# Where a transformer kernel writes its rows of ones, who casts its first two weight slots, and its last four input loads

## What is computed

```
x = x + attn_a(layernorm(x));  x = x + ffn(layernorm(x))
x = x + attn_b(layernorm(x));  x = x + ffn(layernorm(x))
# attn: softmax(causal(q k^T / sqrt(32))) v, 16 heads of 32, then a 512 x 512 projection
# ffn:  (silu(x w_gate^T) * (x w_up^T)) w_down^T, hidden 2048
```

## Time and profile before

| | us |
|---|---|
| median of 3 runs | 2128.01 |
| lowest, highest | 2127.96, 2130.42 |
| the profiled execution | 2130.63 |
| its span, first to last instruction | 2128.9 |
| PE busy | 2062.0 (97%) |
| DVE busy | 1210.9 (57%) |
| POOL busy | 999.1 (47%) |
| ACT busy | 698.6 (33%) |
| store of a tile, issue to landing, median | 2.1 |

### The profile page before, as it was taken

The page is one execution under the profiler, slowest core; times in us unless marked ns, Lnnn a source line. Parts: engine busy times, 40 slices in busy tenths (PEclk is TensorE's granted clock), DMA queues, the critical chain, the costliest instruction groups (busy, mean ns, idle before and its releaser), DMA issues.

```text
span 2128.9 us, 35275 instructions
## 1 busy us (share of the span) xinstructions
PE 2062.0 (97%) x10816; PEld 1443.1 (68%) x10816; DVE 1210.9 (57%) x2452; ACT 698.6 (33%) x1348; POOL 999.1 (47%) x776
## 2 busy tenths in 40 slices
PE   6999999999999999999999999999999999999997
PEld 5555478888755547888875554888877554588886
DVE  6766554454676645544557664555456666454554
ACT  1344432231144443222214444222221444422321
POOL 3323249863312425975331242697533223379752
PEclk9999999999999999999999999999999999999999
DMA  4433101111323210211242321111113232111112
GB/s 129 101 78 83 32 30 50 60 60 40 81 71 81 71 31 30 64 51 55 70 131 71 81 71 31 40 60 50 50 41 85 66 81 71 41 39 62 50 57 92
DMA packets 59756, 135.18 MB, mean 63 GB/s; under 512 B 10784, under 2 KB 11808, under 8 KB 59552
## 3 DMA queue, kind: packets, MB, share of 16 engines
q1 hardware_dynamic: 59552, 132.71, 22.1%
HBM read 77.62 MB, written 4.19 MB: 38 GB/s over the span
## 4 chain that ended last, share of the span: by engine, by line
PE 86%; issue 4%; DVE 3%; POOL 3%; ACT 2%; DMA 1%; SPq 0%; DVEq 0%; POOLq 0%; ACTq 0%
PE bank L1279 13%; PE bank L1166 10%; PE bank L1168 10%; PE bank L1167 10%; PE ring L1166 9%; PE ring L1167 9%; PE ring L1168 9%; PE ring L1233 8%; PE bank L1257 7%; PE ring L1157 1%; POOL area L671 1%; ACT prob L713 1%; DMA area<-nm_lo 1%; POOL area L530 1%; DVE xn L908 1%
## 5 line engine op out<-in xcount | busy, mean ns | idle before, releaser
L713 ACT ACTIVATE prob<-bank 128x512 f32<-128x512 f32 (+3 forms) x768 | 335.0, 489 | 343.6 <-PE bank L1257 342.8
L908 DVE CUSTOM_DVE_ANT_0 xn<-ring,mask_row 128x128 bf16<-128x128 f32 (+7 forms) x512 | 374.8, 749 | 106.4 <-PE ring L1233 99.5
L605 POOL TENSOR_SCALAR_AFFINE_SELECT prob<-prob 128x512 f32<-128x512 f32 x128 | 84.1, 657 | 568.7 <-ACT prob L713 568.7
L528 POOL TENSOR_SCALAR area<-w_stage 128x1024 fp32r<-128x1024 f32 x131 | 149.9, 1144 | 369.3 <-PE bank L1168 194.7
L530 POOL TENSOR_TENSOR area<-w_stage,area 128x1024 fp32r<-128x1024 f32 x131 | 313.9, 2396 | 10.9
L967 DVE TENSOR_TENSOR x<-x,bank 128x512 f32<-128x512 f32 x256 | 170.8, 684 | 233.1 <-PE bank L1168 233.1
L1166 PE MATMUL ring<-xt_hi,area 128*128 128x512 f32 x688 | 273.7, 398 | 4.3 <-DVE xt_lo L880 2.8
L1167 PE MATMUL ring<-xt_lo,area 128*128 128x512 f32 x688 | 269.3, 391 | 0.0
L1168 PE MATMUL ring<-xt_hi,area 128*128 128x512 f32 x688 | 268.9, 391 | 0.0
L1233 PE MATMUL ring<-area 96*128 96x512 f32 (+3 forms) x768 | 239.1, 372 | 9.4 <-DVE row_max L908 8.4
L1233 PEld LDWEIGHTS ring<-area 96*128 96x128 f32 x768 | 131.1, 188 | 151.1 <-DVE row_max L908 94.5
(11 more groups left out here) (144 smaller groups left out, 3233.6 us busy)
## 6 DMA issues: line engine op xcount, KB each, us to landing
w_stage<-ffn_w SPq DMA_DIRECT2D x96, 512.0 KB, 3.3
area<-kq_parts SPq DMA_DIRECT2D x336, 128.0 KB, 2.4
w_stage<-attn_w SPq DMA_DIRECT2D x35, 512.0 KB, 3.2
x<-x_in SPq DMA_DIRECT2D x24, 256.0 KB, 3.9
area<-attn SPq DMA_DIRECT2D x48, 128.0 KB, 2.3
out<-x SPq DMA_DIRECT2D x16, 256.0 KB, 2.1
bias_rows<-row_bias SPq DMA_DIRECT2D x10, 256.0 KB, 4.2
area<-nm_hi SPq DMA_DIRECT2D x32, 8.0 KB, 1.8
```

Of the source, the lines that this page charges most:

```text
L528: pool.tensor_scalar(hi, src, 1.0, 0.0, ALU.mult, ALU.add).then_inc(w_hi_done, 1)
L713: act.activation(prob[:, step % 2, h, off:], bank[n % 2][:, off:], ACT.Exp, scale=SCALE).then_inc(prob_ready, 1)
L908: dve.tensor_tensor_reduce(out=sum_out[:, RING[name] % 2, 0:keys], in0=src[:, 0:keys], in1=mask_row[:, TOKENS - keys:], scale=1.0, scalar= ...
```

## The change

Three edits. **Ones:** VectorE's memset at the start and both memsets of GpSimd are gone; instead GpSimd writes all four buffers with one memset at the head of each iteration, right behind the `rstd` of tiles 4 to 7, for which it waits, and ahead of the split of slot 3. **First two slots:** ScalarE casts their high parts before the loop; GpSimd subtracts the low parts, and only once `xn_ready` says that tiles 0 to 3 are normalised; TensorE waits for slot 0 and slot 1 apart, each where it first uses it. **Input:** the four loads of chunk 1 behind the last batch are gone, SP's outer loop is written out, and SP waits for the stores at its end.

```
-            with sp.Fori(0, BATCH) as b:
+            for b in range(BATCH):
...
-                        if n >= AFTER_STORE:
+                        if n >= AFTER_STORE and not (b == BATCH - 1 and c):
...
-            for s in x_loaded:
-                sp.wait_ge(s, 16 * CT * (BATCH + 1))
+            for c, s in enumerate(x_loaded):
+                sp.wait_ge(s, 16 * CT * (BATCH + 1 - c))
+            for s in x_stored:
+                sp.wait_ge(s, 16 * BATCH)
...
-            split_weights(0, 0)
             inverse_deviation(0, 0, 0)
-            for i in range(1, AHEAD):
+            wait_alone(pool, xn_ready, CT)
+            for i in V_SLOTS:
+                hi, lo = w_part(i, slice(0, SLOT))
+                wait_alone(pool, w_hi_done, i + 1)
+                pool.tensor_tensor(lo, w_stage[:, i, :], hi.bitcast(F32), ALU.subtract).then_inc(w_split, 1)
+            for i in range(len(V_SLOTS), AHEAD):
                 split_weights(0, i)
             with pool.Fori(0, BATCH * LAYERS) as it:
                 inverse_deviation(it, 0, 1)
+                wait_alone(pool, rstd_ready, it * 2 * CHUNKS + CHUNKS)
+                pool.memset(k_stack[3 * HEAD:3 * HEAD + 2, :, :, :].bitcast(F32), 1.0).then_inc(ones_ready, 1)
+                pool.wait_ge(ones_ready, it + 1)
                 split_weights(it, AHEAD)
...
-                pool.memset(k_stack[3 * HEAD:3 * HEAD + 2, 0, :, :].bitcast(F32), 1.0).then_inc(ones_ready, 1)
-                pool.wait_ge(ones_ready, 2 * it + 2)
...
-                wait_alone(pool, product_full, products(it, QUAD_LAST, "m3", 1))
-                wait_alone(pool, w_split, it * SLOTS + SLOTS + 2)
-                pool.memset(k_stack[3 * HEAD:3 * HEAD + 2, 1:, :, :].bitcast(F32), 1.0).then_inc(ones_ready, 1)
-                wait_alone(pool, ones_ready, 2 * it + 3)
...
+            for i in V_SLOTS:
+                act.wait_ge(w_loaded[i], 16)
+                act.activation(w_part(i, slice(0, SLOT))[0], w_stage[:, i, :], ACT.Copy).then_inc(w_hi_done, 1)
...
-            dve.memset(k_stack[3 * HEAD:3 * HEAD + 2, 1:, :, :].bitcast(F32), 1.0).then_inc(ones_ready, 1)
...
-                        pe.wait_ge(w_split, it * SLOTS + V_SLOTS[1] + 1)
+                    if k % 2 == 0:
+                        pe.wait_ge(w_split, it * SLOTS + V_SLOTS[k // 2] + 1)
...
-                        if u in (0, 2):
-                            pe.wait_ge(ones_ready, 2 * it + 1 + u // 2)
+                        if u == 0:
+                            pe.wait_ge(ones_ready, it + 1)
```

## The result

The changed kernel takes 2139.34 us (2138.56 to 2140.64, 6 runs) against 2129.22 us of the kernel before (2127.96 to 2131.87, 6 runs): ratio 1.0045, 95% interval 1.0034 to 1.0056, so some 10 us slower. Its profiled execution has a span of 2137.2 us, 8.3 more than that of before.

A forecast was written before the change was run, and what follows sets the result against it. TensorE's matmuls bound the kernel (86% of the chain), so only its waits count. Heads +27.6, start -5.7 and end -5.0 us make +16.9 on a median of 2128.0: 2145 us, range 2116 to 2150.

The forecast's parts named there:

- The hold: Iteration heads: VectorE's normalisation waits for GpSimd's whole memset, key projection 10.0 us behind the start of `xn`; chance 0.72.
- The clock: Iteration heads: TensorE's clock falls behind the waits, +2.1 us each in iterations 1 and 3, 1.0 in iteration 0.
- The start: Before the first product: normalisation without GpSimd beside it lets that product start at 16.35 instead of 22.04, -5.7 us.
- The end: End of the program: the last store follows at once instead of behind a load, -5.0 us.
- The sum: Whole kernel: 27.6 - 5.7 - 5.0 = +16.9 us, so 2145 us.
- Rival (1): Iteration heads: the memset does not hold VectorE up, as it reads nothing; only the gains stand, 2117.3 us; chance 0.20.
- Rival (2): Heads: held, but one tile passes first and the clock stays up in iterations 0, 1, 3; 2138 us; no separate chance.
- Rival (3): Heads: TensorE gets only the transposes late and something else loses its wait, loss of 6 to 15 us; chance 0.05.
- rival (4): Start: the gain fails, slot 1's low part or ScalarE's cast being late; at most 5.7 us back, 2151; chance 0.03.

The follow-up runs named there:

- e1: The changed kernel, but GpSimd's memset of ones waits until tiles 4 to 7 are normalised; 2115.73 us, ratio 0.9936 to the kernel before.
- e3: The changed kernel, but VectorE normalises tiles 4 to 7 with a two-tensor scalar_tensor_tensor, memset still behind rstd; 2120.71 us, ratio 0.9951 to the kernel before.
- e10: The changed kernel with half of the memset behind rstd and the other half behind the normalisation; 2127.31 us, ratio 0.9989 to the kernel before.
- e4: The kernel before with the edit on the ones alone; 2151.45 us, ratio 1.0095 to the kernel before.

## Why the prediction was right, and where it was off

**The hold.** Right, and shown by e1, e3 and e10: the first `tensor_scalar` waits for the whole memset and 0.28 us more. The 10.0 us from the start of `xn` to the key projection is 9.98 in iterations 0, 1 and 3 and 9.96 in iteration 2 (562.11 - 552.13 in iteration 1). The losses of time alone were forecast as 3.4, 6.1, 6.8 and 6.1; by the distances they are 3.4, 6.1, 6.7 and 5.6. The last is smaller because iteration 3 of before does not repeat iteration 1: its key projection starts 4.4 us behind `xn`, not 3.9.

**The clock.** The term that was mis-sized, with iteration 2. For iterations 1 and 3 I took 2.1 us each from iteration 2 of before; they took 1.5. For iteration 0 I took 1.0: there was none, although TensorE waited 1.85 and 1.07 us there; behind the same waits in e4 it was 1.5, so the half that I took is not refuted. In iteration 2 the twelve matmuls took 4.08 us instead of 4.94, so the clock came back sooner than before, behind a longer wait. I had 5.2 us for the clock, and the traces give 0 + 1.5 - 0.9 + 1.6 = 2.2. I had also held fixed what VectorE waits for ahead of `xn`: in iteration 2 it waited 2.91 us for its input instead of 3.83, and in iteration 1 `xn` came 0.4 us earlier against TensorE than before. The heads cost 22.7 us by the traces, 23.6 by the medians against e1, and I had 27.6.

**The start.** -6.8 instead of -5.7. The first product came 5.0 us earlier and not 5.7; 0.4 of that is the input, which landed at 7.0 and not 6.6. Another 1.8 us came from the full clock of the first nine matmuls, which I had left out. That part is luck: e3 has the same start, its first matmuls ran at the lower clock, and it is 5.05 us ahead in the second value tile, where e1 is 7.0. That ScalarE's casts and the later subtractions are hidden was right (1.06 us each).

**The end.** -5.2 for -5.0.

**The sum.** +16.9 was forecast, +9.6 measured by the ratio; the terms by the traces, 22.7 - 6.8 - 5.2, make 10.7. The sign, the place and the mechanism held; of the gap, 4.9 us are too much at the heads and 1.3 too little at start and end. The stated range, 2116 to 2150, was wide, since it took in most of both outcomes; the own range of the hold, 2137 to 2150, has 2139.3 near its lower end.

**The rivals.** Rival (1), that the memset does not hold VectorE up, is refuted by the row of 7.3 us. Its price was about right: e1 and e3, where nothing is held at the heads, take 2116 and 2121 us, and it had 2117. VectorE does not pass all four tiles first; not even one passes. Rival (2) had 2138, nearer to the measured 2139.3 than my 2145, but for another reason: it let one tile pass and the clock stay up in iterations 0, 1 and 3. No tile passed, and the clock fell in 1 and 3. Rival (3), a loss and a gain that meet, and rival (4), a failed start, did not occur.

## What to carry to other kernels

In this kernel a GpSimd instruction that was free on its own list held up a VectorE `tensor_scalar` from SBUF to SBUF by its whole length. For another kernel: ask what VectorE does on the same semaphore, and let GpSimd wait for the end of it, not for its start. Cutting the instruction up into as many parts as VectorE had instructions did not help; moving it 2 us did, and 23 us came back. Of a change with parts of both signs, run each part alone: here two good edits of 6 and 7 us were hidden under a bad one of 20, whose memset only had to start later.

## What I had not expected of the hardware

VectorE's first normalisation starts, by its row, 0.08 us ahead of the memset (24.98 and 25.06), and yet it is the one that waits, at the head of every iteration. And the clock: in the profiled execution of before it fell to 0.66 and 0.57 in two windows in which TensorE was busy all the time (5.00 of 5.00 and 3.92 of 4.00 us), without a wait ahead that would explain it: TensorE's waits just ahead were under 0.5 us, and as long in the changed kernel, where the same work ran at 1.00. Behind the same wait of 0.92 us before the first product, e1's ran at full clock (0.49) and e3's at the lower (0.79); behind the same waits at the head of iteration 0, the changed kernel's twelve matmuls took 2.90 us and e4's 4.36. A term for the clock behind a short wait is thus uncertain by its own size, 1.5 to 2 us each time; why it falls in one run and not in another stays open.
